# Order of the split products in each large tile of a Mamba-2 layer: both products of one stationary high part behind each other

## The reference, cut to what matters

```python
xn = layernorm(x)                                 # (2, 1024, 512)
proj = einsum('bld,pd->blp', xn, in_proj_w)       # gate | x, B, C | dt
xBC = silu(causal_conv_4_taps(proj[..., hbc]) + conv_bias)
dt_p = softplus(dt + dt_bias); dA = exp(dt_p * A)
state = state * dA_t + dtx_t * B_t                # 64 heads of 64 x 128, a step per token
y_t = einsum('bhpn,bhn->bhp', state, C_t)
y = y + x * D
yn = y * rsqrt(mean(y * y over a group of 512)) * norm_weight * silu(gate)
s = einsum('bli,di->bld', yn, out_proj_w)         # (2, 1024, 512)
g = silu(xn @ W.T + bias + lora(xn))
out = x + s * g
```

## Time and profile before

| what | value |
|---|---|
| runs | 1794.21, 1794.66, 1797.45 us, median 1794.66 |
| span of the profiled execution | 1793.2 us, from the first to the last instruction |
| its own time with what lies around the span | not listed by itself; the span is 1.0 us under the lowest run |
| granted clock of PE, mean | 0.998 of 2.4 GHz |
| PE busy | 1759.6 us, 98%, 11416 matmuls and as many weight loads |
| DVE, POOL, ACT busy | 85%, 64%, 47% |

### The profile page before, as it was taken

How to read it: one execution, slowest core, us unless ns; L and a number is a source line. 1 busy time by engine, 2 the same in 40 slices (tenths; PEclk the granted TensorE clock), 3 DMA queues, 4 the chain that set the end, 5 groups by cost and what they waited for, 6 DMA issues and landing times.

```text
span 1793.2 us, 30683 instructions
## 1 busy us (share of the span) xinstructions
PE 1759.6 (98%) x11416; PEld 1417.5 (79%) x11416; DVE 1522.7 (85%) x1936; ACT 836.0 (47%) x1923; POOL 1145.6 (64%) x1143
## 2 busy tenths in 40 slices
PE   8999999999999999999999999999999999999997
PEld 5778878888887888888777788888888888888875
DVE  7868888888888888888888988889898888989887
ACT  4554453544435354443534434354444535444465
POOL 6537566565756656575697847648574664757567
PEclk9999999999999999999999999999999999999999
DMA  8533333232332323333574333323233332324234
GB/s 267 159 124 113 123 98 133 100 108 105 106 130 87 137 107 106 106 107 124 172 233 143 120 110 127 109 95 123 90 119 117 114 122 94 119 94 129 95 112 147
DMA packets 113508, 220.78 MB, mean 123 GB/s; under 512 B 10448, under 2 KB 46672, under 8 KB 113360
## 3 DMA queue, kind: packets, MB, share of 16 engines
q1 hardware_dynamic: 112320, 218.66, 36.2%
q10 hardware_dynamic: 1040, 0.16, 0.0%
HBM read 204.63 MB, written 14.16 MB: 122 GB/s over the span
## 4 chain that ended last, share of the span: by engine, by line
PE 83%; DVE 8%; ACT 4%; issue 2%; POOL 2%; DMA 1%; SPq 0%; ACTq 0%; DVEq 0%; POOLq 0%
PE ps_conv L1304 9%; PE ps_conv L1307 9%; PE ps_y L1478 6%; PE ps_conv L1310 6%; PE ps_out L1304 6%; PE ps_out L1307 6%; PE ps_gate L1304 6%; PE ps_gate L1307 6%; PE ps_y L1483 5%; PE ps_s L1515 5%; PE ps_out L1310 4%; PE ps_gate L1310 4%; PE turned_x L1395 3%; DVE xc L885 2%; PE ps_conv L1311 2%
## 5 line engine op out<-in xcount | busy, mean ns | idle before, releaser
L885 DVE SCALAR_TENSOR_TENSOR xc<-ps_conv,convw_sb,xc 128x511 f32<-128x511 f32 (+2 forms) x576 | 430.3, 747 | 153.9 <-ACT xc L651 140.3
L1237 POOL TENSOR_TENSOR rstd_col<-mean_square,half 128x1 f32<-128x1 f32 x128 | 89.4, 698 | 533.2 <-ACT mean_square L794 533.2
L1009 DVE TENSOR_TENSOR_SCAN decay<-decay,eye 128x1024 f32<-128x1024 f32 x125 | 294.7, 2358 | 0.9 <-DMA decay<-decays_d 0.9
L657 ACT ACTIVATE xc<-xc 128x512 f32<-128x512 f32 x192 | 121.0, 632 | 322.0 <-DVE xc L885 320.6
L1226 POOL TENSOR_TENSOR cpre<-cpre,xc 128x1024 f32<-128x1024 f32 x112 | 268.8, 2400 | 0.0
L1304 PE MATMUL ps_conv<-xn_hi,wconv_hi 128*128 128x512 f32 x768 | 242.0, 437 | 0.0
L1307 PE MATMUL ps_conv<-xn_hi,wconv_lo 128*128 128x512 f32 x768 | 207.4, 392 | 0.0
L1478 PE MATMUL ps_y<-decay,dtx 128*64 128x128 f32 x1984 | 190.9, 279 | 3.6 <-DVE decay L1030 2.8
L1304 PEld LDWEIGHTS ps_conv<-xn_hi,wconv_hi 128*128 128x128 f32 x768 | 141.4, 194 | 49.3 <-issue 27.2
L803 ACT ACTIVATE square<-ps_y 128x512 f32<-128x512 f32 x126 | 75.6, 600 | 220.8 <-DVE ps_y L1062 220.8
L1483 PE MATMUL ps_y<-cpre,state 128*64 128x128 f32 x1760 | 171.3, 273 | 0.0
(11 more groups left out here) (241 smaller groups left out, 3860.4 us busy)
## 6 DMA issues: line engine op xcount, KB each, us to landing
decay<-decays_d SPq DMA_DIRECT2D x125, 512.0 KB, 5.4
cpre<-rows_d SPq DMA_DIRECT2D x112, 512.0 KB, 3.9
stage<-w_in_t SPq DMA_DIRECT2D x32, 1024.0 KB, 6.6
stage<-w_out_t SPq DMA_DIRECT2D x16, 1024.0 KB, 5.5
stage<-w_in_t SPq DMA_DIRECT2D x32, 256.0 KB, 3.1
out_sum<-hidden SPq DMA_DIRECT2D x16, 256.0 KB, 5.6
ffn_d<-sgate SPq DMA_DIRECT2D x16, 256.0 KB, 2.8
out<-out_sum SPq DMA_DIRECT2D x16, 256.0 KB, 3.6
```

The lines of the kernel that those rows point to most:

```text
L885: e.scalar_tensor_tensor(acc[:, d:], ps[:, 0:BLK - d], convw_sb[:, tile, TAPS - 1 - d:TAPS - d], acc[:, d:], ALU.mult, ALU.add).then_inc(S ...
L1009: e.tensor_tensor_scan(d, d, eye8[:, :, :].rearrange("p h i -> p (h i)"), 0.0, ALU.mult, ALU.add).then_inc(scanned(i)[0], 1)
```

## The change

In `passes` the loop over the contracted blocks now issues high x high and, right behind it, stationary high x moving low of the same block; the stationary operand of such a pair is the same. The four products with the stationary low part come last. `third` (the wait for the moving low part) moves from ahead of the ninth matmul to ahead of the second, and `second` (the wait for the stationary low part) from ahead of the fifth to ahead of the ninth. The number of matmuls and the place of the increment at the twelfth stay.

```diff
                 (a_hi, a_lo), (b_hi_, b_lo_) = a, b
                 for t in range(n):
                     e.matmul(ps, a_hi(t), b_hi_(t), start=t == 0, stop=False)
+                    if t == 0:
+                        third()
+                    e.matmul(ps, a_hi(t), b_lo_(t), start=False, stop=False)
                 second()
-                for t in range(n):
+                for t in range(n - 1):
                     e.matmul(ps, a_lo(t), b_hi_(t), start=False, stop=False)
-                third()
-                for t in range(n - 1):
-                    e.matmul(ps, a_hi(t), b_lo_(t), start=False, stop=False)
-                e.matmul(ps, a_hi(n - 1), b_lo_(n - 1), start=False, stop=True).then_inc(done, 1)
+                e.matmul(ps, a_lo(n - 1), b_hi_(n - 1), start=False, stop=True).then_inc(done, 1)
```

## The result

| what | before | after |
|---|---|---|
| median of 5 runs each, us | 1794.66 | 1802.18 |
| lowest and highest, us | 1793.64 to 1797.45 | 1799.35 to 1803.32 |
| span of the profiled execution, us | 1793.2 | 1800.8 |
| mean granted clock in it | 0.998 | 0.996 |

The ratio is 1.0036, with a 95% interval of 1.0024 to 1.0049: slower by about 0.4%, 7.5 us by the medians. The forecast was 3.8 us slower (1798.5), and 1802.18 lies above its range, which ended at 1801.0. The profiled execution after the change took 1802.65 us, 1.8 us more than its span; it is 0.5 us above the median. Both profiled spans differ by 7.6 us, and these 7.6 us are what has to be found.

The account below looks back on a forecast made before the run. The prediction took PE, busy 98% of the span, as the bound. Its terms, 0 + 0 + 1.26 + 1.61 + 0.92 = +3.8 us on the median of 1794.66, gave 1798.5 us, with a range of 1795.4 to 1801.0.

Parts of the forecast that it names:

- Step 1: All tiles: pairs sharing a stationary operand change neither the number of loads nor the spacing of products, 0 us.
- Rival C: All tiles: the load is skipped or shortened for a repeated stationary operand, up to 28 us gained, about 1770; chance 0.05.
- Step 2: Main loop: the moved waits for low parts cost 0 us; the wait for ynt_lo can give 0.5 us at most.
- Step 3: Prologue: waiting for xn_lo ahead of the second product costs +1.26 us in the third rate tile, +1.61 in the fourth.
- Rival A: Fourth rate tile: the clock falls to 1.2 GHz behind PE's wait, another 1.7 us, 1800.2 us; chance 0.20.
- The cover: Prologue: PE's 1.9 us of waits for xn_lo hide the first two rate tiles' losses of 1.6 us each.
- Step 4: Last output tile: the sum of squares is issued behind eight products, not four, and the end comes 0.92 us later.
- Rival B: Between 57 and 81 us DVE swallows the third rate tile's 1.26 us; 2.5 us remain, 1797.2 us; chance 0.22.
- rival D: Prologue and tail: the waits are hidden and nothing visible changes, 1794.7 us; chance 0.11.

Follow-up runs that it names:

- prologue_and_last_old: The changed kernel with the former order in the rate tiles, the linear tiles and the last output tile: 1794.45 us, ratio 0.9998 to the kernel before.
- fill_waits: The changed kernel with 8, 8 and 10 useless copies of the first product ahead of it in the first, third and fourth rate tile: 1799.88 us.
- before_fill_gate: The kernel before with nine useless products ahead of the third gate tile: 1794.60 us, ratio 0.9999.
- rates_behind: The changed kernel, third and fourth rate tile issued behind conv and linear tile, former order in first rate and linear tiles, last sum of squares earlier: 1793.69 us.
- rates_behind_fill: rates_behind with nine useless products ahead of the third gate tile: 1793.63 us, ratio 0.9992 to the kernel before.
- only_rate_new: The kernel before with the paired order in the four rate tiles alone: 1798.95 us, ratio 1.0023.
- prologue_fifth: The changed kernel, but rate and linear tiles wait for the moving low part ahead of the fifth product, last output tile in former order: 1796.92 us.

## Why the prediction was right in sign and wrong in size

**Step 1, the order itself, 0: right.** The 112 steps from the eighth to step 120 take 1476.2 us in either order, and prologue_and_last_old isn't told apart from before. Rival C, the load skipped or shortened, is out: 11416 loads for 11416 products, at 188 ns and 0.23 us as before.

**Step 2, waits in the main loop, 0: right** within 0.5 us, and in part by luck. L1030 is 6.35 us late at the first step, 6.58 at step 8 and 6.81 at the last. The first 0.2 us arise between step 0 and step 1 and were not traced to a cause. The second are the fourth fall, shown above. The prediction had the wait for ynt_lo as a thing that could only give, up to 0.5 us; its idle time went into the next wait, and the clock fell behind that. It cost little only because PE isn't the bound there.

**Step 3, the rate tiles, +1.26 and +1.61: this is the step that failed.** The prologue's shift in the profiled pair, by tile:

| place | shift of PE there, us | what the prediction had |
|---|---|---|
| start of the third rate tile | +1.21 (55.51 to 56.72) | 0, covered |
| this tile | +3.50 | +1.26 |
| fourth rate tile | +3.23, to +7.93 at the conv tile (82.86 to 90.79) | +1.61 |
| third gate tile and on to the first matrix | -1.6, to +6.35 | 0 |

It failed at two points, both the clock's; a third difference comes from the execution that was traced:

- **No term for the clock.** In the third and fourth tile 1.6 us each are the fall of the clock. Rival A named this mechanism, priced it rightly at 1.7 us, and asked for it behind one wait only. The text gave it 0.20 as something that might happen at the fourth tile, and did not ask the same of the first and third, whose waits came out at 1.7 us. The untraced runs agree: of the changed kernel's five, four took 1801.72 to 1803.32 us at mean clocks of 0.995 and 0.996, and the fifth 1799.35 at 0.998. Against them stands one fall fewer: the kernel before had its own at the third gate tile, and the changed kernel's traced execution has the same wait there without a fall. In the timeline of PE:

```profile
115.28 0.50 PE L1304 MATMUL ps_y<-xn_hi,wgate_hi 128*128 128x512 f32 x1 [2.08 <-ACT sgate L715]
115.62 0.39 PE L1307 MATMUL ps_y<-xn_lo,wgate_hi 128*128 128x512 f32 x1
```

- **The cover was sized for a tile without a fall.** The first two rate tiles' loss was to vanish in PE's 1.9 us of waits ahead of 55.13, and 1.21 us came through. The prediction's own figures don't fit here either: two losses of 1.6 us are 3.2, more than 1.9. The first tile lost 3.2 by itself, wait and fall, and the second 0.6, since it started 2.2 us late and then waited only 0.42. The cover took 1.6 us, for the shift was 2.80 behind the second rate tile and 1.21 at the third. In fill_waits, where the first tile has no fall, the shift is 1.54 behind the second tile and none at the third. So the 1.21 us too are the clock's. The reason given, that DVE works on without a break, does not hold: DVE itself waits here for a conversion of ACT that hangs on PE's turned tokens, in DVE's timeline after the change:

```profile
35.15 0.69 DVE L875 TENSOR_TENSOR xn_lo<-turned_x,xn_hi 128x512 fp32r<-128x512 f32 x1 [1.22 <-ACT xn_hi L702]
```

- **The third tile, 1.90 instead of 1.26.** PE starts the tile 1.21 us later, and xn_lo comes 1.76 later. These 0.55 us are one instruction of DVE, right ahead of xn_lo: L864 at 57.10 took 1.09 us (above), and in the kernel before, at 55.90, 0.54. POOL's timeline says what else differed, before:

```profile
56.01 1.04 POOL L1127 TENSOR_TENSOR wconv_lo<-stage,wconv_hi 128x256 fp32r<-128x256 f32 x1
```

and after:

```profile
57.20 0.72 POOL L1127 TENSOR_TENSOR wconv_lo<-stage,wconv_hi 128x256 fp32r<-128x256 f32 x1
```

The two overlap in both kernels, and one of them is long: POOL's before, DVE's after. In prologue_and_last_old, whose rate tiles have the former order, DVE's is the long one as well (1.12 and POOL's 0.73), so this isn't the order's doing. In before_fill_gate, whose instructions up to the third gate tile are those of the kernel before, it is too:

```profile
56.16 1.12 DVE L864 TENSOR_SCALAR out_sum<-out_sum,mean_var,rstd 128x512 f32<-128x512 f32 x1
```

There PE starts the conv tile behind the fourth rate tile at 83.68, 0.82 us later than the trace of before (82.86). So this is a difference between executions and no fault of the prediction, which could read only the one trace; of the twelve traces here three have DVE's short (before, rates_behind, rates_behind_fill). It also means that a part of the 7.6 us belongs to this pair of executions. The kernel only_rate_new, in which DVE's is long too (1.09), confirms 1.9 and 1.6 us for the two tiles without falls.

**A step was missing.** The list of callers had the linear tiles, and the sum had no word on them. Their wait for wout_lo is hidden in the changed kernel behind the first rate tile's delay. So it adds no row of its own to the 7.6 us, but it is why restoring the rate tiles alone left 1.4 us in the prologue.

**Step 4, the last output tile, +0.92: right.** The sum of squares is issued behind eight products and not four, and the tail is 0.85 us longer. In the timeline of the tail, beside the earlier trace rows:

```profile
1794.72 0.26 ACT L794 ACTIVATE mean_square<-ps_g,eps 128x1 f32<-128x1 f32 x1 [2.00 <-PE ps_g L1297]
1794.88 0.62 ACT L844 ACTIVATE stage<-stage 128x512 f32<-128x512 f32 x1
...
1795.54 0.69 DVE L978 TENSOR_TENSOR out_sum<-out_sum,stage 128x512 f32<-128x512 f32 x1 [1.28 <-ACT stage L844]
```

DVE waits 1.28 us for the silu where it waited 0.39, which is 0.89 us more.

**Sum in hindsight:** 1.21 carried, 1.90 + 1.60 for the third tile, 1.63 + 1.60 for the fourth, -1.6 at the gate tile, 0.46 between the first and the last matrix (0.24 of it the fourth fall), 0.85 in the tail: 7.65, and the rounded spans differ by 7.6. Without the clock's parts in the prologue (1.21 + 1.60 + 1.60 - 1.6 = 2.8) it is 4.8, an estimate that lies within the range given; the forecast sum was 3.8. Rival B, the delay swallowed by DVE between 57 and 81, is out, since xn_lo of the fourth tile came 4.75 us later; and so is rival D.

**What stays open.** What decides whether the clock falls behind a given wait: the idle time in brackets doesn't do it alone. The wait of 1.66 us at 59 us was followed by a fall in the changed kernel and not in only_rate_new, the one of 2.08 us before the third gate tile was followed by a fall before the change and not after, and one of 0.88 us was enough in prologue_fifth. Nor is it seen where the clock falls in executions that were not traced, or why fill_waits gained 4.8 us on the changed kernel in the span of its profiled execution and only 2.3 us in its median; the mean clock doesn't settle it. The 7.6 us are taken apart for one pair of traces, and their parts would come out otherwise in another pair.

## What to carry to other kernels

Reordering the terms of a sum also moves the waits of their operands: put the terms whose operands are written last at the end of the tile, because each product that comes to stand behind a wait is added to its cost. A helper that is free in its steady loop must be costed at every other caller too, where the operands are fresh (prologue, first use of a weight, last step). Where PE has to idle for a late operand near the critical path, put other tiles ahead of it, as rates_behind does, since an idle of 2 us can cost another 1.6 us of slow clock behind it. And compare more than one trace of the same code before an instruction's length is put down to a change.

## What the runs showed of the hardware beyond what was expected

- Waits of PE of 1.66 to 2.19 us, and one of 0.88 (prologue_fifth), were followed by a stretch at 1.2 GHz with 0.43 us per product, and each such stretch cost about 1.6 us where PE was full. The kernel before had one in its traced prologue, the changed one three there and one near the end of the main loop.
- It isn't the same in every execution of a kernel or at every wait of a length, so that the mean granted clock, 0.995 to 0.998 in the changed kernel's runs and 0.998 to 1.000 in those of the kernel before, was the only mark of it in the runs without a trace.
- Useless products in a wait can shorten a kernel: 26 more of them took 4.4 us off the changed kernel's prologue in the traced execution, and 2.3 us off the median.
- Two neighbouring products with the same stationary operand were neither slower nor faster than two with different ones, to within 0.1 us over the 1476.2 us from the eighth step to step 120.
- An instruction of DVE (L864) and one of POOL (L1127) that overlap: 0.54 and 1.04 us in the trace of before, 1.12 and 0.74 in that of before_fill_gate, whose instructions are the same up to there. Which of the two is the long one can shift an operand by half a microsecond.
